# A transformer layer on one core: where a few transposes, weight presets, copies and clamps are issued

## The reference

```python
def bitnet_linear(x, weight, scale_param):
    s = maximum(mean(abs(weight), axis=1), 1e-08)
    y = einsum('bsi,oi->bso', x, sign(weight / s[:, None])) * (s * scale_param)
    return nan_to_num(y, nan=0.0, posinf=1e6, neginf=-1e6)

q, k, v = bitnet_linear(xn, ...)        # 32 query heads, 8 key/value heads, 32 wide
attn = softmax(q @ k.T / sqrt(32))      # 1024 x 1024 for each head and batch
attention = bitnet_linear(attn @ v, o_weight, o_scale)
ffn = (silu(xn @ gate) * (xn @ up)) @ down   # weights 4 bit, (w - zero) * scale in groups of 128 rows
```

## Time and profile before

| | |
|---|---|
| median of 3 runs | 2307.51 us (2306.16 to 2314.76) |
| profiled execution | 2308.84 us, of which the span is 2307.0 us |
| TensorE busy | 2254.0 us (98%) |
| VectorE, ScalarE, GpSimd busy | 1800.1 (78%), 1580.1 (68%), 1023.1 us (44%) |
| mean granted TensorE clock | 0.996 |
| chain that ended last | PE 88%, SP's queue 4%, VectorE 3%, DMA 2% |

### The profile page before, as it was taken

One profiled execution on the slowest core, in us unless ns is written; L12 is line 12 of the kernel. 1 busy time (PEld: TensorE's weight loads), 2 busy tenths in 40 slices (PEclk: granted clock), 3 DMA queues, 4 the chain that ended last, 5 costly groups with the idle time before them and its releaser, 6 DMA issues.

```text
span 2307.0 us, 44216 instructions
## 1 busy us (share of the span) xinstructions
PE 2254.0 (98%) x18068; PEld 1008.6 (44%) x18068; DVE 1800.1 (78%) x2301; ACT 1580.1 (68%) x2047; POOL 1023.1 (44%) x574
## 2 busy tenths in 40 slices
PE   6999999999999999999999999999999999999998
PEld 4444344443444444334444444444445444444444
DVE  8878888888888888766677777777777777777776
ACT  6763888888888888852466666666666666666665
POOL 0000799999899999943155553210003222221001
PEclk9999999999999999999999999999999999999999
DMA  5352445445444454449678886131114111115111
GB/s 189 89 122 94 108 107 118 102 110 116 100 115 109 103 122 106 102 126 192 159 94 95 95 97 79 37 119 37 37 65 146 37 37 47 45 37 183 37 37 73
DMA packets 206447, 220.56 MB, mean 96 GB/s; under 512 B 105170, under 2 KB 144978, under 8 KB 205222
## 3 DMA queue, kind: packets, MB, share of 16 engines
q1 hardware_dynamic: 135542, 163.21, 23.0%
q0 software_dynamic: 70704, 54.53, 19.0%
HBM read 164.28 MB, written 69.64 MB: 101 GB/s over the span
## 4 chain that ended last, share of the span: by engine, by line
PE 88%; SPq 4%; DVE 3%; DMA 2%; ACT 1%; issue 1%; DVEq 0%; POOL 0%; ACTq 0%
PE ps L1798 34%; PE ps L1814 17%; PE ps L1555 8%; PE ps L1614 8%; PE ps L1628 8%; PE ps L1767 5%; PE ps L1584 4%; PE ps L1645 3%; SPq L412 2%; DMA zone<-zone_c 1%; DVE sm L1072 1%; SPq L438 1%; ACT zone L886 1%; PE ps L1831 0%; DVE zone L1209 0%
## 5 line engine op out<-in xcount | busy, mean ns | idle before, releaser
L1798 PE MATMUL ps<-xT,zone 128*128 128x512 f16 x3584 | 774.2, 379 | 0.0
L1231 DVE TENSOR_REDUCE zone<-ps 128x1 f32<-128x512 f32 x1024 | 636.4, 681 | 109.8 <-PE ps L1555 105.5
L886 ACT ACTIVATE zone<-ps,sm 128x512 f32<-128x512 f32 x1024 | 624.4, 695 | 99.4 <-PE ps L1614 96.3
L700 POOL TENSOR_TENSOR xT<-zone 128x1024 f32<-128x1024 f32 x252 | 616.0, 2663 | 156.4 <-ACT zone L886 156.4
L1470 DVE TENSOR_SCALAR ps<-ps,zone_c 128x1024 f32<-128x1024 f32 x392 | 506.7, 1293 | 162.4 <-PE ps L1798 160.3
L1011 ACT ACTIVATE ps<-ps,zone_c 128x1024 f32<-128x1024 f32 x392 | 426.5, 1088 | 248.3 <-PE ps L1798 248.3
L1798 PEld LDWEIGHTS ps<-xT,zone 128*128 128x128 f16 x3584 | 350.6, 98 | 422.5 <-DVE zone L1474 0.3
L1614 PE MATMUL ps<-zone 98*32 98x512 f16 x4096 | 413.0, 381 | 10.1 <-DMA zone<-zone_c 5.5
L1555 PE MATMUL ps<-zone 96*32 96x512 f16 (+1 forms) x3946 | 412.7, 382 | 8.5 <-DVE zone L1231 8.5
L1814 PE MATMUL ps<-zone 128*128 128x512 f16 x1792 | 387.1, 379 | 0.0
L1481 DVE TENSOR_SCALAR ps<-ps,zone_c 128x1024 f32<-128x1024 f32 x216 | 279.2, 1293 | 93.1 <-PE ps L1814 92.9
(11 more groups left out here) (143 smaller groups left out, 1377.5 us busy)
## 6 DMA issues: line engine op xcount, KB each, us to landing
zone<-dequantised SPq DMA_DIRECT2D x84, 512.0 KB, 3.6
xT<-xT POOLq DMA_DIRECT2D x31, 1024.0 KB, 9.1
dequantised<-zero_points SPq DMA_DIRECT2D x84, 256.0 KB, 4.1
zone<-zone SPq DMA_DIRECT2D x384, 32.0 KB, 1.9
zone<-_attn_hidden_states_dram SPq DMA_DIRECT2D x16, 512.0 KB, 6.4
zone<-inverse_sums SPq DMA_DIRECT2D x128, 64.0 KB, 2.5
attention<-zone SPq DMA_DIRECT2D x32, 256.0 KB, 6.1
xT<-attention SPq DMA_DIRECT2D x4, 2048.0 KB, 12.0
```

What stands on the lines that cost most here:

```text
L700: nc.gpsimd.tensor_tensor(pairs[:, j, hp, :], prob[:, prob_slot(e), :], prob[:, prob_slot(e + 2), :], add).then_inc(s["sum_ok"], 1)
L886: A(prob[:, prob_slot(e), m % 2 * 512:(m % 2 + 1) * 512], ps[:, 3 + m % 3, :], ACT.Exp, scale=gam[:, 0:1]).then_inc(s["exp_ok"], 1)
L1231: V.tensor_reduce(mxs[:, u % 2, half, i % 16:i % 16 + 1], ps[:, (2 * i + half) % 3, :], AX, amax).then_inc(s["max_ok"], 1)
L1798: last = MM(ps[:, 4 * s2 + 2 * m + c, :], ring[:, buf, m * H + g * P:m * H + (g + 1) * P], xT[:, hf, part, g, c * 512:(c + 1) * 512], star ...
```

## The change

Four edits. On SP's queue the transposes of tiles 12 to 15 are issued ahead of `load_q(1)` and `load_k(1)` instead of behind them. The presets no longer come at every sixth step: three a unit are issued at k = 9, 12 and 15 of units 0 to 27, behind `load_m`. The copies `evacuate_values(30)`, `evacuate_sums(30)` and `evacuate_values(31)` go from ScalarE to VectorE, and `head_of(29)` goes from k = 14 of the last unit to the output projection, n = 2. At the start of the attention `keep_numbers` of the last projection runs in step 1 ahead of `row_max(26)` instead of in step 2 behind `row_max(27)`, and the first of the two last pairs of head and tail in step 4 instead of 5.

```diff
@@ SP
             load_q(0)
+            for i in range(12, 16):
+                turn_tile(i)
             load_q(1)
             load_k(1)
-            for i in range(12, 16):
-                turn_tile(i)
             load_q(2)
@@ SP, for e in range(STEPS)
-                if e % 6 == 0 and e // 6 < TILES:
-                    preset_weights(e // 6)
...
                 if k == 8 and u + 1 < UNITS:
                     load_m(u + 1)
+                if k in (9, 12, 15) and 3 * u + (k - 9) // 3 < TILES:
+                    preset_weights(3 * u + (k - 9) // 3)
@@ ScalarE, for e in range(STEPS)
-                elif e in (5, 7):
-                    head(NC - 1, 10 + (e - 5) // 2)
-                if k == 0 and u:
+                elif e in (4, 7):
+                    head(NC - 1, 10 + (e - 4) // 3)
+                if k == 0 and 1 <= u < UNITS - 1:
                     evacuate_values(u - 1)
-                if k == 5 and u:
+                if k == 5 and 1 <= u < UNITS - 1:
                     evacuate_sums(u - 1)
-                if k == 14 and u >= 2:
+                if k == 14 and 2 <= u < UNITS - 1:
                     head_of(u - 2)
...
-            evacuate_values(UNITS - 1)
             output_signs(1)
...
                 if n == 1:
                     evacuate_sums(UNITS - 1)
+                elif n == 2:
+                    head_of(UNITS - 3)
@@ VectorE
+            def evacuate_values(u):
+                dve.wait_ge(s["pv_pe"], round_of(u, 7) + 1)
+                dve.wait_ge(s["ol_ok"], u - 2)
+                V.tensor_copy(num[u % 3], ps[:, 6, :]).then_inc(s["ev_ok"], 1)
+
+            def evacuate_sums(u):
+                dve.wait_ge(s["dn_pe"], ones_before(u + 1))
+                dve.wait_ge(s["mu_ok"], u - 1)
+                V.tensor_copy(den[:, u % 2, :], ps[:, 7, :]).then_inc(s["evd_ok"], 1)
...
+                if e == 1:
+                    keep_numbers(NC - 1, 11)
                 if e + LEAD < STEPS:
                     row_max(e + LEAD)
                 if e == 0:
                     clamp_output(NC - 1, 11)
-                elif e == 2:
-                    keep_numbers(NC - 1, 11)
-                elif e in (5, 7):
-                    tail(NC - 1, 10 + (e - 5) // 2)
+                elif e in (4, 7):
+                    tail(NC - 1, 10 + (e - 4) // 3)
...
                 if u == UNITS - 1:
+                    if k == 1:
+                        evacuate_values(u - 1)
+                    elif k == 5:
+                        evacuate_sums(u - 1)
...
+            evacuate_values(UNITS - 1)
             for j in (2, 3):
```

## The result

The changed kernel took 2294.24 us in the median of 7 runs (2292.98 to 2301.38), beside 2311.6 us of the kernel before in 7 runs on the same chip. The ratio is 0.9934, with a 95% interval of 0.9918 to 0.9951: 15 us less.

The account below looks back on a forecast made before the run. TensorE, busy almost everywhere, was taken as the bound, so only isolated holes and the lower clock behind them could be won: 7.8 + 6.5 + 0.9 + 1.0 = 16.2 us off 2308.84, giving 2292.6 us, range 2289 to 2298.

Parts of the forecast that it names:

- A: Earlier transposes close TensorE's 4.84 us hole near 168 us and avoid 2.96 us of lower clock: 7.8 us.
- Both sub-steps: Near 168 us: `low(14)` starting 5.1 us sooner covers the 4.84 us hole; the clock staying up saves 2.96 us.
- B: Presets out of SP's way in the attention: fewer key-score waits for the maxima's DMA and less lost clock, 6.5 us.
- the waits of L1614 for the maxima's DMA near zero: Sign in the attention: key scores hardly wait for the maxima, whose waits were 5.3 us, every pair issued before its join.
- the shift of 0.6 to 1.2 us: On SP's queue, the maxima's pair moves forward this much where two presets stood ahead, or one in an even chain.
- That pulls three of the four pairs out of the join's way: Three of four late maxima pairs escape GpSimd's 1 MB transfer; the one near 443 us keeps about 0.5 us of wait.
- C: Last unit: two ScalarE copies removed from among the exponentials, worth 0.5 and 0.4 us, 0.9 us together.
- D: First attention steps: VectorE's copy gains 0.5 us, step 4's tail 1.1, step 7's tail loses 0.6: 1.0 us.
- The slower one: Attention: presets in a row hold up the join; over 0.5% slower from 1.0 us past its slack per unit; chance 0.05.
- The rival that the pairs still meet the join: Attention: SP's lateness at the maxima's pair comes from issue times and waits, not presets; 2299.1 us, chance 0.08.

Follow-up runs that it names:

- e1: Kernel before with only the transposes of tiles 12 to 15 moved ahead of the second query and key loads: ratio 0.9969, 7.2 us less.
- e2: Kernel before with only the presets moved behind the maxima's DMAs: ratio 0.9977, 5.3 us less.
- e11: Changed kernel with the presets back at every sixth step, leaving transposes, copies and clamps: 2299.71 us, ratio 0.9959 to the kernel before.
- e3: Kernel before with only the last units' copies on VectorE and the first clamps one step ahead: ratio 0.999, 2.3 us less.
- e4: Changed kernel with SP issuing the maxima's pair ahead of the four denominator DMAs: 2356.28 us, ratio 1.0195 to the kernel before.
- e5: Changed kernel with the 12 query DMAs of unit u + 3 issued behind the maxima's pair: 2324.22 us, ratio 1.0064 to the kernel before.

## Why the prediction was right

It said 2292.6 us, and 2294.24 was measured; in ratios 0.9930 (2292.6 / 2308.84) and 0.9934. (The distances below combine to 5.0 us by root of the sum of squares, not 5.1; that changes nothing.) The terms:

- **A, 7.8 us.** The trace gives 8.07, the times of e1 7.2. Both sub-steps held: `low(14)` at 159.0 instead of the forecast 159.1, no hole, and the clock at 1.00 in the window behind it. SP's later query loads cost nothing.
- **B, 6.5 us.** e2 gives 5.3 and e11 against the changed kernel 5.8, so the size is right within its error. The picture behind it was not, and that the number fits is in part luck. The prediction expected one pair to stay late and "the waits of L1614 for the maxima's DMA near zero"; the profiled execution had three such waits and 6.5 us, the second one and 2.2 us, and e2 four and 6.4 us. The step that failed is "That pulls three of the four pairs out of the join's way", with the shift of 0.6 to 1.2 us ahead of it. In even units, where nearly all waits are, the pairs moved by 0.1 to 0.2 us on average and stayed behind the join. The boundary that the prediction shows, in unit 13, is the only one of the 21 waits of the old order that lies in an odd unit, where the edit does work. It also read four late pairs of one execution as fixed places. Which pairs are late varies: among the four of the kernel before, only the one in unit 16 was late in all five traces of the old order. The traces fit an edit that makes late pairs rarer (2.7 instead of 4.2 a trace, waits of 5.0 instead of 7.2 us), but the ranges overlap, and even at 1.6 us of time for each of waiting that is 3.4 of the 5 us. Where the rest of B's gain comes from is open.
- **C, 0.9 us.** The last unit gives 0.51, in e3 as well (25.19 us long), where the two copies were put at 0.9. The sum is right only if the 0.4 of the wait in the output projection is counted, which the prediction did not have and which e1 lacks without the copies. So this term was about twice too large.
- **D, 1.0 us.** 1.15 measured in holes. The copy took 0.74 instead of 2.30 and waited 1.17 for the mask (foreseen 1.0). The tail in step 4 ran free (0.75 instead of the 1.3 assumed), and the tail in step 7 was held (1.77 instead of 0.74). The copy and the free tail had no GpSimd addition beside them, so 2.30 us was not the copy's own length. In some executions the clock falls here: 0.92 in the changed kernel's first profile, 1.00 in its second. This was not in the sum.
- **The rivals.** The slower one did not come, though its mechanism did: the join's landing went from 9.1 to 10.0 us in the median (8.1 to 12.2), within the slack of about 3 us. No engine waited for a join in either profile of the changed kernel. The rival that the pairs still meet the join is there in both profiles of the changed kernel as a mechanism, while the median, 2294.24 us, lies 5 us below its 2299.1.

## What to carry to other kernels

A queue that issues in order has a deadline at each entry, and what can be moved is only what has none; before moving an entry forward or back, write down the reader of each entry that is shifted, since another reader may have less slack than the one that is late now (e4), and a long stretch of issue may be the cover of a round trip (e5). When a small transfer shares the DMA engines with a large one, the distance between the two issues decides, so change that distance from either side, measure it pair by pair, and look at more than one profile: a wait that one trace shows may be absent from the next execution of the same program. Count a TensorE hole at more than its length where the rows behind it show the lower clock.

## What the runs showed of the hardware

A small transfer of 4 KB from SP lands 1.7 us after issue in the median (4.5 at most) when it leaves ahead of the 1 MB accumulating transfer from GpSimd, and after 5.3 to 8.6 us when it leaves 0.9 us or more behind it (390 pairs in 13 traces). In the changed kernel, both DMAs of all pairs:

```profile
DMA to landing us min/median/max: 1.6/1.7/8.6
```

A preset lands after 4.1 us in the median in the kernel before, one at a time, and after 6.5 and 7.2 us in the two profiles of the changed kernel, where most go out in trains. The join lands after 9.9 to 10.0 us in the median in the three profiles with these trains, and after 9.0 to 9.3 in the five with presets at every sixth step. TensorE's clock did not answer to every hole in the same way: behind waits of 2.0 and 2.87 us the stretches show 0.93 and 0.91, behind other waits of 2.0 and 1.6 us 1.00, and in the first attention steps the same program had 0.92 in one execution and 1.00 in the next.
